# Chunked linear attention in halves of 64 tokens: units of 8 heads, column tiles, a redrawn order

## The chip, the cores and the metric
The kernel runs on one core of one Trainium2 chip. The metric is the device time of one execution in microseconds, the median of several runs. The core has TensorE (matrix products, PE in the profile, its weight loads PEld), VectorE (DVE), ScalarE (ACT), GpSimd (POOL) and SyncE (SP), which here issues every DMA.

## The reference, cut to what matters
The input is x of 4 sequences x 1024 tokens x 256 features. Three layers follow each other: half an FFN (routed to one of 8 experts by low-rank terms), an attention layer with a gated MLP, half an FFN again. Each starts from a layer norm. The change touches the recurrence of the attention, with 16 heads of 16 features:

```
def step(carry, inp):
    C, n = carry
    qt, kt, vt, it, ft = inp
    C = ft[:, :, None, None] * C + it[:, :, None, None] * (vt[..., :, None] * kt[..., None, :])
    n = ft[..., None] * n + it[..., None] * kt
    ht = jnp.einsum('bhde,bhe->bhd', C, qt)
    denom = jnp.maximum(jnp.abs(jnp.einsum('bhd,bhd->bh', n, qt)), 1.0)[..., None]
    return ((C, n), ht / denom)
```

i_gate is exp(clip(h @ wi + bi)), f_gate is sigmoid(h @ wf + bf). The result y goes through wo and is added to the layer's input; then come a norm and silu(h2 @ w_gate) * (h2 @ w_up) @ w_down.

## The kernel before, in words
Tokens go in 8 blocks of 512, two blocks a sequence, a block in 4 chunks of 128. RUNS lists the runs of work: "1" and "2" are the two FFNs, "A" the projections of the attention, "L" the gated MLP, each for one block. In the steady part a round is L of one block, 1 of the block three later, A of the block two later, 2 of the first. The attention of a block goes on between its A and its L, in steps put between those of the runs.

Every engine executes a fixed list. Its steps are generators with one-letter names, and ORDER says, for each engine, which generator takes the next step ("3U" is three steps of U). Each step waits for semaphores of the others. So what stands ahead in an engine's list must be done before what stands behind it.

On TensorE: U makes up-projections and the attention's projections into two PSUM banks (product(), lines 1044 to 1046, three matmuls of float32 halves that stand for one precise product). V makes down-projections. G transposes normed inputs and computes routing (line 1216, on column tiles of 32). S, M and Y are the attention.

The recurrence is computed by chunks. A unit is 4 heads of a chunk (QUAD, NQ = 4 units a chunk, 128 units in all).
- E (SP) broadcasts the running products of the forget gates from DRAM to the tile dm, on all partitions. D (VectorE, line 979) turns them by a scan into the matrix of decay between tokens, 128 x 512.
- S (TensorE, line 1236) multiplies keys and queries, one 128 x 128 matrix a head, in bfloat16 parts stacked to 96 rows. P (VectorE, line 990) multiplies by dm into pt.
- M (TensorE, line 1255) multiplies pt by the gated values with one more column for the denominator (vp, 17 columns), on four column tiles of 32 tokens. After the fourth unit the state of the chunks before is added to the same bank M by two full-width matmuls (line 1269, carry) with q scaled by cumE; a chunk that opens a sequence has none.
- Y: wv (GpSimd, line 562) is vp weighted by the decay to the chunk's end. Line 1282 multiplies k by wv, all heads with all heads, into bank W; lines 1004 and 1007 (VectorE) mask the blocks of a head with itself; lines 576 and 581 (GpSimd) decay the old state and add the new. A chunk that closes a sequence makes no state. Then VectorE divides (lines 1012 to 1022, y), TensorE transposes y (line 1289), ScalarE and VectorE split it (lines 757 and 1026), TensorE multiplies by wo (the same lines 1044 to 1046), VectorE adds it to z (line 1030). One bank W serves state, transpose and output product of a chunk, so the next state waits for z.

The forget products are scanned over 128 tokens at line 875; the input gate is one exp on ScalarE for a block, and vp is written at line 881, one instruction for two chunks. r_h and r_l are the two halves of an FFN's hidden activations: ScalarE writes r_h (line 624), VectorE r_l (line 807), and V waits for both. u_st holds the low-rank part of an FFN's input in two buffers.

Of the kernel before, what the change touches and what calls it, by code (L numbers as in the profile page):

```python
# [7 lines left out]
P = 128  # L8
N_SEQ, SEQ, D = 4, 1024, 256
TILES = 4  # L10
# [5 lines left out]
F = 1024  # L16
# [10 lines left out]
NQ = H // QUAD  # L27
UNITS = TILES * NQ
# [37 lines left out]
class Run:  # L66


    def __init__(self, i):
# [19 lines left out]
        2G 2U 2G 3U V 2U V U V U V 4U V 2U V U 2V 2G 6U G 2U 2G U G 7U V 2U V U V U V 3U 2S U V 2U V U V 2S 2M Y V 2S 2M S Y M S M G Y S G 2U S M 2U M 2U S M  # L89
        Y U S G U Y 2M G S Y U S 2M U G U S U M G Y 3U Y U S V M U M U Y V 2M U M V Y U V Y 2U Y U 2S U V 2U V G U V 2S 2M V 2U G 2U V 2U 2S 3M V 2U V G 2S Y  # L90
        2U G Y M V U G U V U S G M Y M V 4U V 2U V U V U V 3U G U V 2U V U G 2V 2U S 2U S M 2U G S Y U M U M Y G M S M Y S 2M G U Y G 2U S 3U S U M U V U M Y
        U V M Y M U M V U V Y 2U Y U S U V 2U V G U V S V 2U G 2U V 2U V S 2U V S M G M Y 2U G V U G U V U G 2S 2M V 4U V 2U V U V U V 3U G U V 2U V U G 2V 2U
        S 2U S Y 2U G 2M U Y 2S 2M U G M Y 2S G Y 2M G U Y U S U S U 2M 2U 2S M Y 2U V Y M U M U Y V 2M U M V Y U V Y 2U Y 2U V 2U V U V G 2S Y V 2U G 2U V 2U
        V 2U V 2S 2M G 2U G S V U G U V U G S 3M V 4U V 2U V U V U V 3U G U V 2U V U G 2V 2U S 2U S Y 2U G 2M U Y 2S 2M U G Y M 2S G M Y M G U Y U S U S 3U 3M
        Y S U S U V M U M Y U V M Y M U M V U V Y 2U Y 2U V 2U V U V G 2S V 2U G 2U V 2U 2S V 2U V 2M Y G 2U G 2S V U G U V U G 2M V 4U V 2U V U V U V 3U G U
        V 2U V U G 2V 2U S 2U S Y 2U G M U M Y S M S U M G M Y 2S G Y 2M G U Y 2U S U M 3U Y S 2M U S Y V M 2U S M Y V M U V 2M Y U V Y 3U S Y U V 2U V U V G
        2S M V 2U G 2U V 2U V 2U V 2S 2M G 2U G S V U G U V U G S 2M V 3U Y U V 2U V U V U V 3U G U V 2U V U G 2V 2U S 2U Y M 2U G S M U Y S M U M Y G M 2S M
        Y G M G 2U S U Y U S 2U 3M Y 2U 2S V M U M Y U V M Y M U M V U V Y 3U S Y U V 2U V U V S G V S 2U G S U M U M V 2U S M V U V U G 2U V 2U G V 2U S V S
        Y M 4U S Y 2M U S M U G S M S M G Y S Y U G Y 2M 2U G U Y S M 3U Y U S 2M V 2U S Y M S M V Y S M U V S 2M Y U V U Y U S U Y S U M V M S 2U M V G S 2M
        S U V Y U S V Y 2M U S Y M U Y G S 2M U V S M Y 2U S M Y V 2U S M V Y S M S M U M Y U V S M Y U 3M U Y V Y V G 4U G U V U V U V U G 2U G V U G U V U G  # L100
# [1236 lines left out]
```

## Time and profile before

| | us |
|---|---|
| median of 3 runs | 987.48 (985.0 to 989.41) |
| the profiled execution | 983.92 |
| its span on the core | 982.1 |
| TensorE busy | 904.4 |
| VectorE busy | 716.5 |
| ScalarE busy | 353.3 |
| GpSimd busy | 247.2 |

The span reaches from the first to the last instruction. A busy time is the union of an engine's instructions, waiting left out. Matmuls overlap each other, so the mean of one is longer than what it takes from the engine; where costs count, starts are compared. A float32 matmul stands in the records twice, a bfloat16 or float32r one once. A granted clock of 1.00 is the upper of TensorE's two levels, 2.4 GHz; the lower is 1.2 GHz.

### The profile page before, as it was taken

How to read it: one execution, taken by the hardware profiler on the slowest of the kernel's cores; microseconds unless marked ns; L12 is line 12 of the kernel's file. 1: busy time of each engine (PE TensorE's matmuls, PEld its weight loads, DVE VectorE, ACT ScalarE, POOL GpSimd, SP SyncE). 2: the span in 40 equal slices, each digit the busy share in tenths (PEclk: the TensorE clock that was granted, in tenths of full speed). 3: DMA queues.
4: the chain of work that ended last, by engine and by line, in shares of the span. 5: the costliest groups of instructions: out<-in, count | busy, mean ns of one | idle time of the engine just before them, and what ended most of it. 6: DMA issues, size and time to landing. Idle time of an engine off the chain costs nothing.

```text
span 982.1 us, 29559 instructions
## 1 busy us (share of the span) xinstructions
PE 904.4 (92%) x12008; PEld 865.6 (88%) x12008; DVE 716.5 (73%) x1516; ACT 353.3 (36%) x692; POOL 247.2 (25%) x285
## 2 busy tenths in 40 slices
PE   3957889999899998999999999999999989997998
PEld 2857889999789997999889997999989978987998
DVE  6634798985857859786787859887688888895642
ACT  5452251433415352343514433252423341313431
POOL 1021252320431123321412304411323143411100
PEclk9877989999999999999999999999999989998999
DMA  8105455220452126330462105531353156510000
GB/s 289 56 16 147 130 148 150 76 74 5 124 139 69 52 61 167 104 85 23 120 172 85 51 24 157 148 90 30 83 161 119 36 161 175 152 46 1 2 21 23
DMA packets 73077, 92.67 MB, mean 94 GB/s; under 512 B 10638, under 2 KB 47246, under 8 KB 72944
## 3 DMA queue, kind: packets, MB, share of 16 engines
q1 hardware_dynamic: 72944, 90.80, 33.0%
q8 instruction: 96, 1.57, 0.7%
q14 instruction: 37, 0.30, 0.1%
HBM read 73.46 MB, written 17.30 MB: 92 GB/s over the span
## 4 chain that ended last, share of the span: by engine, by line
PE 69%; DVE 11%; SPq 8%; issue 6%; DMA 3%; ACT 2%; POOL 1%; DVEq 0%; ACTq 0%; POOLq 0%
PE bank L1044 19%; PE bank L1046 18%; PE bank L1045 18%; SPq L425 5%; PE bank L1079 3%; PE bank L1255 3%; PE bank L1202 2%; PE bank L1236 2%; DMA dm<-f_scratch 2%; DVE dm L979 2%; SPq L443 1%; PE bank L1269 1%; DVE pt L990 1%; PE bank L1282 1%; DVE a_st L892 1%
## 5 line engine op out<-in xcount | busy, mean ns | idle before, releaser
L624 ACT ACTIVATE r_h<-bank 128x512 fp32r<-128x512 f32 x128 | 76.4, 598 | 280.3 <-PE bank L1079 280.2
L979 DVE TENSOR_TENSOR_SCAN dm<-dm,ident 128x512 f32<-128x512 f32 x128 | 159.7, 1254 | 22.9 <-DMA dm<-f_scratch 22.6
L1044 PE MATMUL bank<-wo_hi,r_h 128*128 128x256 f32 x512 | 147.2, 287 | 4.3 <-DVE r_l L807 4.0
L1044 PE MATMUL bank<-xT_hi,wi_hi 128*128 128x256 f32 x512 | 148.6, 290 | 1.9 <-DVE r_l L807 1.5
L1045 PE MATMUL bank<-wo_hi,r_l 128*128 128x256 f32 x512 | 144.5, 282 | 0.0
L1046 PE MATMUL bank<-wo_lo,r_h 128*128 128x256 f32 x512 | 144.4, 282 | 0.0
L1046 PE MATMUL bank<-xT_lo,wi_hi 128*128 128x256 f32 x512 | 144.4, 282 | 0.0
L1045 PE MATMUL bank<-xT_hi,wi_lo 128*128 128x256 f32 x512 | 144.2, 282 | 0.0
L807 DVE SCALAR_TENSOR_TENSOR r_l<-bank,r_h 128x512 fp32r<-128x512 f32 x128 | 87.5, 684 | 77.4 <-ACT r_h L624 76.8
L562 POOL TENSOR_TENSOR wv<-vp,dm 128x68 f32<-128x68 f32 x128 | 49.8, 399 | 245.9 <-DVE dm L979 132.5
L1044 PE MATMUL bank<-xT_hi,wgu_hi 128*128 128x256 f32 x352 | 102.7, 292 | 2.4 <-DVE xT_lo L941 2.1
L1044 PEld LDWEIGHTS bank<-wo_hi,r_h 128*128 128x128 f32 x512 | 97.2, 190 | 5.5 <-issue 5.2
L1044 PEld LDWEIGHTS bank<-xT_hi,wi_hi 128*128 128x128 f32 x512 | 97.7, 191 | 3.8 <-DVE r_l L807 3.3
L1045 PE MATMUL bank<-xT_hi,wgu_lo 128*128 128x256 f32 x352 | 99.6, 283 | 0.0
L1046 PE MATMUL bank<-xT_lo,wgu_hi 128*128 128x256 f32 x352 | 99.4, 282 | 0.0
L1045 PEld LDWEIGHTS bank<-xT_hi,wi_lo 128*128 128x128 f32 x512 | 97.8, 191 | 0.0
L1046 PEld LDWEIGHTS bank<-xT_lo,wi_hi 128*128 128x128 f32 x512 | 97.5, 190 | 0.0
L1046 PEld LDWEIGHTS bank<-wo_lo,r_h 128*128 128x128 f32 x512 | 97.3, 190 | 0.0
L1045 PEld LDWEIGHTS bank<-wo_hi,r_l 128*128 128x128 f32 x512 | 97.2, 190 | 0.0
L990 DVE TENSOR_TENSOR pt<-bank,dm 128x512 f32<-128x512 f32 x128 | 85.7, 681 | 10.4 <-PE bank L1255 9.1
L519 POOL TENSOR_TENSOR g_rs<-g_ve,minus_half 128x4 f32<-128x4 f32 x24 | 29.2, 1216 | 230.4 <-DVE g_ve L920 218.5
L1044 PEld LDWEIGHTS bank<-xT_hi,wgu_hi 128*128 128x128 f32 x352 | 67.5, 192 | 3.6 <-issue 1.7
(158 smaller groups left out, 2198.7 us busy)
## 6 DMA issues: line engine op xcount, KB each, us to landing
dm<-f_scratch SPq DMA_DIRECT2D x128, 256.0 KB, 4.4
arena<-parts_scratch SPq DMA_DIRECT2D x96, 128.0 KB, 3.5
arena<-parts_scratch SPq DMA_DIRECT2D x96, 64.0 KB, 3.7
arena<-parts_scratch SPq DMA_DIRECT2D x32, 192.0 KB, 3.9
x<-in_x SPq DMA_DIRECT2D x16, 256.0 KB, 3.0
parts_scratch<-pa SPq DMA_DIRECT2D x64, 64.0 KB
parts_scratch<-pb SPq DMA_DIRECT2D x64, 64.0 KB
parts_scratch<-pc SPq DMA_DIRECT2D x64, 64.0 KB
```

The source lines that it names most:

```text
L425: sp.dma_start(to, part[:, x % 2, jj * DC * P:(jj + 1) * DC * P]).then_inc(d_parts[x % 2], 16)
L519: nc.gpsimd.tensor_tensor(g_rs[:], g_ve[:], minus_half[:, 0:TILES], ALU.pow).then_inc(g_rstd, 1)
L562: nc.gpsimd.tensor_tensor(wv[:, heads], vp[:, b % 2, j, heads], w, ALU.mult).then_inc(a_wv, 1)
L624: nc.scalar.activation(flat(r_h[:, n]), U[use % 2][:], ACT.Relu).then_inc(f_rh, 1)
L807: v.scalar_tensor_tensor(r_l[:, n].rearrange("p a t -> p (a t)"), U[use % 2][:], 0.0, r_h[:, n].rearrange("p a t -> p (a t)").bitcast(F32) ...
L979: v.tensor_tensor_scan(dm[:, g], dm[:, g], ident4[:], 0.0, ALU.mult, ALU.add).then_inc(a_D, 1)
L990: v.tensor_tensor(pt[:, u % 2], S[u % 2][:], dm[:, u % NQ], ALU.mult).then_inc(a_P, 1)
L1044: nc.tensor.matmul(dst, lh, rh, start=first, stop=False, **more)
L1045: nc.tensor.matmul(dst, ll, rh, start=False, stop=False, **more)
L1046: return nc.tensor.matmul(dst, lh, rl, start=False, stop=last, **more)
L1079: done = nc.tensor.matmul(dst, lora_b[0:LS2, cols], u_st[0:LS2, r.k % 2, h * HALF:(h + 1) * HALF], start=False, stop=True, skip_group_chec ...
L1255: done = nc.tensor.matmul(M[tile, h * HV:(h + 1) * HV], pt[:, u % 2, i * P + q * P // COLS:i * P + (q + 1) * P // COLS], vp[:, b % 2, j, h ...
```

## The change
A chunk of 128 tokens is split into two halves of 64 (TH). Decay, scores and values are made within a half; what the second half takes from the first goes through the state. A unit is now 8 heads of a chunk (GH), 64 units in all. In bank S, partitions 0 to 63 hold the first half and 64 to 127 the second, each head 64 columns.
- S: for each head four matmuls on column tiles of 32 keys, with the 64 queries of their own half.
- M: heads in pairs; two tiles take one head, two the other, and the values vq have both halves side by side with zeros in the other half's rows, 34 columns. The clearing of vq is one memset on GpSimd at the start. There are three buffers of two chunks.
- The forget products are scanned and stored by halves, the input gate is four small exp instructions a block instead of one, the value product two instructions of 64 partitions instead of one.
- State: k by wv on four column tiles, each with its own two heads, 68 columns, for every chunk. VectorE makes from it the state at the chunk's half (c_at[1]) and at its end (c_at[0]), two small instructions each. GpSimd spreads each by head (c_ex) under the mask.
- Carry: for each half four column tiles x two groups of features, so 16 matmuls of 68 columns a chunk, 8 in an opening one. It waits for this chunk's own first state and spread.
- dm has three buffers, y and u_st one; wo's rows are loaded in another order, and yT is written by halves.
- ORDER is redrawn on all engines; the steps of U, V and G are the same in number.

Core of the diff:

```
+TH = P // 2
+GH = 8
+NG = H // GH
+UNITS = TILES * NG
+DMBUFS = 3
+VBUFS = 3
...
+        vq = sb("vq", [P, VBUFS, 2, H, 2, HV])
...
+                        src = f_d[b % 2, j, :, GH * g:GH * (g + 1)].rearrange("m h t -> m (h t)")
+                        sp.dma_start(dm[:, n % DMBUFS], src.unsqueeze(1).to_broadcast([2, TH, GH * TH])).then_inc(d_fb[n % DMBUFS], 16)
...
+                nc.gpsimd.memset(vq[:], 0.0).then_inc(s_zero, 1)
...
+                        w = dm[:, n % DMBUFS].rearrange("p (h t) -> p h t", h=GH)[:, :, TH - 1:TH].to_broadcast([P, GH, 2 * HV])
...
+                def spread(n):
+                    pairs = HH // 2
+                    nc.gpsimd.tensor_tensor(c_ex[n][:].rearrange("p c (q d) -> p c q d", q=pairs),
+                                            c_at[n][:].unsqueeze(2).to_broadcast([P, DC, pairs, 2 * HV]),
+                                            headmask[:].rearrange("p (q d) -> p q d", q=pairs).unsqueeze(1).to_broadcast([P, DC, pairs, 2 * HV]),
+                                            ALU.mult).then_inc(a_ex[n], 1)
...
+                    pool.wait_ge(a_at[1], DC * (n + 1))
+                    pool.wait_ge(a_c, n)
+                    spread(1)
...
+                        pool.wait_ge(a_at[0], DC * n_on(b, j))
+                        pool.wait_ge(a_c, n + 1)
+                        spread(0)
...
+            def input_gates(b, h):
+                half = 2 * b + h
+                if half >= VBUFS:
+                    act.wait_ge(a_wv, NG * 2 * (half - VBUFS + 1))
+                    act.wait_ge(a_O, NG * 2 * (half - VBUFS + 1))
...
-                        if r.k > 1:
-                            of = FFN_RUN[r.k - 2]
+                        if r.k:
+                            of = FFN_RUN[r.k - 1]
...
+                    for c in range(DC):
+                        if opens(b, j):
+                            done = v.tensor_scalar(two(c_at[1][:, c]), added[:, c, :, 0], 1.0, None, ALU.mult)
+                        else:
+                            done = v.scalar_tensor_tensor(two(c_at[1][:, c]), two(c_at[0][:, c]), end(c, 0), added[:, c, :, 0],
+                                                          ALU.mult, ALU.add)
+                        done.then_inc(a_at[1], 1)
...
+                        for i in range(GH):
+                            h = place_of(GH * g + i)
+                            for q in range(COLS):
+                                tile = slice(q * P // COLS, (q + 1) * P // COLS)
+                                own = slice(q // 2 * TH, (q // 2 + 1) * TH)
+                                done = nc.tensor.matmul(S[n % 2][tile, i * TH:(i + 1) * TH], ks[:, j % 2, h, tile], qs[:, j % 2, h, own],
+                                                        start=True, stop=True)
...
+                        for i in range(GH // 2):
+                            pair = GH // 2 * g + i
+                            for q in range(COLS):
+                                tile = slice(q * P // COLS, (q + 1) * P // COLS)
+                                of = (2 * i + q // 2) * TH + q % 2 * (P // COLS)
+                                done = nc.tensor.matmul(M[tile, pair * 2 * HV:(pair + 1) * 2 * HV], pt[:, n % 2, of:of + P // COLS],
+                                                        values(b, j)[:, 2 * pair + q // 2].rearrange("p m d -> p (m d)"),
+                                                        start=pair == 0, stop=False, skip_group_check=True)
...
+                        pe.wait_ge(a_ex[1], c_n + 1)
+                        pe.wait_ge(a_qc, DC * (b + 1))
+                        if not opens(b, j):
+                            pe.wait_ge(a_ex[0], n_on(*chunks[c_n - 1]))
...
+                                    of = c_ex[m][:, c].rearrange("p (h e d) -> p h e d", e=2, d=HV)[:, :, q // 2]
+                                    done = nc.tensor.matmul(heads[tile, HH // 2 * c:HH // 2 * (c + 1), m], q32[:, b % 2, c, t:t + P // COLS], of,
+                                                            start=False, stop=True, skip_group_check=True)
...
+                            done = nc.tensor.matmul(W[tile, c * 4 * HV:(c + 1) * 4 * HV], k32[:, b % 2, j, of:of + P // COLS],
+                                                    wv[:, HH * c + 2 * q:HH * c + 2 * q + 2].rearrange("p h m d -> p (h m d)"),
+                                                    start=True, stop=True)
```

## Rows read from the trace of the kernel before

**Rows 1.** The page's first lines: the span, and TensorE's busy time.
```profile
span 982.1 us, 29559 instructions
...
PE 904.4 (92%) x12008; PEld 865.6 (88%) x12008; DVE 716.5 (73%) x1516; ACT 353.3 (36%) x692; POOL 247.2 (25%) x285
```

**Rows 2.** Stretches: from:to, length, busy us by engine, clock, DMA share, GB/s.
```profile
0.00:112.00 112.00, 77.01 (x652) 72.94 (x653) 62.07 (x131) 46.24 (x89) 17.85 (x20) 0.86 0.41 124
112.00:860.00 748.00, 717.57 (x10129) 686.83 (x10129) 584.14 (x1239) 272.35 (x539) 214.84 (x251) 0.98 0.37 102
```

**Rows 3.** Waits of TensorE: who waited for whom, us in total, times, longest.
```profile
PE bank L1236 <- DVE pt L990: 5.1, 4, 1.5
PE bank L1289 <- DVE y L1022: 4.4, 6, 1.2
```

**Rows 4.** Timeline, an M unit among products: start us, us, instruction, count.
```profile
758.60 0.28 PE L1046 MATMUL bank<-xT_lo,wgu_hi 128*128 128x256 f32 x1
758.81 0.45 PE L1255 MATMUL bank<-vp,pt 128*32 128x17 f32 x32
...
759.41 0.28 PE L1045 MATMUL bank<-xT_hi,wgu_lo 128*128 128x256 f32 x1
```

**Rows 5.** Timeline, an S unit among products, and two S units in a row.
```profile
605.59 0.28 PE L1046 MATMUL bank<-wkv_lo,xT_hi 128*128 128x256 f32 x1
605.72 0.40 PE L1236 MATMUL bank<-arena 96*128 96x128 bf16 x4
...
606.12 0.28 PE L1045 MATMUL bank<-xT_hi,wi_lo 128*128 128x256 f32 x1
...
536.32 0.62 PE L1236 MATMUL bank<-arena 96*128 96x128 bf16 x8
```

**Rows 6.** Timeline, a state step among products.
```profile
396.86 0.28 PE L1046 MATMUL bank<-wo_lo,r_h 128*128 128x256 f32 x1
396.98 0.62 PE L1282 MATMUL bank<-wv,k 128*128 128x136 f32 x4
...
397.56 0.28 PE L1045 MATMUL bank<-xT_hi,wi_lo 128*128 128x256 f32 x1
```

**Rows 7.** Lines 1255 and 1216: ns min/median/max, first and last start; a routing group.
```profile
L1255 PE MATMUL bank<-vp,pt x4096: 177/183/238, 112.7 to 884.0; 128*32 128x17 f32 x196
...
L1216 PE MATMUL bank<-route_w,xn x1024: 196/202/277, 19.1 to 945.4; 128*32 128x40 f32 x171
...
664.32 0.80 PE L1216 MATMUL bank<-route_w,xn 128*32 128x40 f32 x64
```

**Rows 8.** VectorE's groups by line: count, busy us, mean ns, idle us before.
```profile
L979 DVE TENSOR_TENSOR_SCAN dm<-dm,ident 128x512 f32<-128x512 f32 x128 | 159.7, 1254 | 22.9 <-DMA dm<-f_scratch 22.6
L990 DVE TENSOR_TENSOR pt<-bank,dm 128x512 f32<-128x512 f32 x128 | 85.7, 681 | 10.4 <-PE bank L1255 9.1 <-PE bank L1236 0.8
L881 DVE TENSOR_TENSOR vp<-bank,vp 128x512 f32<-128x512 f32 x16 | 10.8, 678 | 2.9 <-PE bank L1046 2.8
L1014 DVE SCALAR_TENSOR_TENSOR den<-bank,den 128x16 f32<-128x16 f32 x32 | 5.6, 175 | 1.1
```

**Rows 9.** GpSimd's groups by line, the same columns.
```profile
L562 POOL TENSOR_TENSOR wv<-vp,dm 128x68 f32<-128x68 f32 x128 | 49.8, 399 | 245.9 <-DVE dm L979 132.5 <-PE bank L1282 60.6 <-issue 33.2
L581 POOL TENSOR_TENSOR cb<-cm,cbd 128x272 f32<-128x272 f32 x24 | 18.8, 784 | 10.6 <-DVE cm L1007 6.4 <-DVE dm L979 3.4 <-issue 0.8
L576 POOL TENSOR_TENSOR cbd<-cb,cumE 128x272 f32<-128x272 f32 x24 | 16.4, 683 | 8.3 <-DVE cb L1004 3.7 <-DMA cumE<-c_scratch 2.1 <-POOL cb L581 0.4
```

**Rows 10.** Timeline of the first microseconds.
```profile
1.44 0.91 DVE L771 MEMSET u_st<- 32x1024 f32 x1 [0.27 <-issue]
...
5.69 1.02 POOL L519 TENSOR_TENSOR g_rs<-g_ve,minus_half 128x4 f32<-128x4 f32 x1 [4.85 <-DVE g_ve L920]
```

**Rows 11.** Timeline of a chunk's end: denominator to y, transpose to the split.
```profile
386.36 0.16 DVE L1012 TENSOR_SCALAR den<-bank 128x16 f32<-128x16 f32 x1
...
387.05 0.42 DVE L1022 TENSOR_TENSOR y<-bank,den 128x256 f32<-128x256 f32 x1
...
388.88 0.38 PE L1289 MATMUL bank<-ident,y 128*128 128x128 f32 x2
...
389.70 0.42 DVE L1026 TENSOR_TENSOR yT_lo<-bank,yT_hi 128x256 fp32r<-128x256 f32 x1 [0.23 <-ACT yT_hi L757]
```

More of the change, by code:

```diff
@@ L210, in build @@
         u_rep = sb("u_rep", [P, TILES, 3, ER])
[L211 removed]
+        u_st = sb("u_st", [P, BLOCK], F32R)
         r_h = sb("r_h", [P, 2, 2, HALF], F32R)
@@ L339, in build @@
         upto = lambda b, j: chunks[:b * TILES + j + 1]
-        n_carry = lambda b, j: sum(not opens(*c) for c in upto(b, j))
-        n_state = lambda b, j: sum(not closes(*c) for c in upto(b, j))
-        n_cb = lambda b, j: sum(not closes(*c) and not opens(*c) for c in upto(b, j))
+        n_on = lambda b, j: sum(not closes(*c) for c in upto(b, j))
         def n_ml(l, s):
@@ L686, in projections @@
                     act.wait_ge(d_f, 16 * TILES * b)
-                nc.scalar.copy(fTz[:, 1:P], bank(A_F)[:, 1:P]).then_inc(a_fTs, 1)
+                halves = lambda t: t.rearrange("p (m t) -> p m t", m=2)[:, :, 1:TH]
+                nc.scalar.copy(halves(fTz[:]), halves(bank(A_F)[:, 0:P])).then_inc(a_fTs, 1)
                 yield
+                input_gates(b, 1)
+                yield
+            def input_gates(b, h):
[3 more added lines that the diff above has]
+                    act.wait_ge(a_O, NG * 2 * (half - VBUFS + 1))
+                else:
+                    act.wait_ge(s_zero, 1)
+                for m in range(2):
+                    rows = slice(m * TH, (m + 1) * TH)
+                    nc.scalar.activation(vq[rows, half % VBUFS, :, :, m, HD], g32[rows, 2 * h:2 * h + 2, 0:H], ACT.Exp).then_inc(a_i, 1)
             def G_():
@@ L874, in projections @@
                     dve.wait_ge(d_c, 16 * TILES * b)
-                v.tensor_tensor_scan(cum[:], bank(A_F)[:, 0:P], zero[:].to_broadcast([P, P]), 1.0, ALU.mult, ALU.add).then_inc(f_read, 1)
+                for m in range(2):
+                    t = slice(m * TH, (m + 1) * TH)
+                    done = v.tensor_tensor_scan(cum[:, t], bank(A_F)[:, t], zero[:].to_broadcast([P, TH]), 1.0, ALU.mult, ALU.add)
+                done.then_inc(f_read, 1)
                 yield
@@ new lines, in Y_ @@
+                    yield
+                    if not closes(b, j):
+                        dve.wait_ge(d_ce, 16 * DC * (b + 1))
+                        dve.wait_ge(a_at[1], DC * (n + 1))
+                        dve.wait_ge(a_ex[0], n_on(*chunks[n - 1]) if n else 0)
+                        for c in range(DC):
+                            v.scalar_tensor_tensor(two(c_at[0][:, c]), two(c_at[1][:, c]), end(c, 1), added[:, c, :, 1],
+                                                   ALU.mult, ALU.add).then_inc(a_at[0], 1)
+                        yield
@@ L1258, in M_ @@
                         done.then_inc(a_O, 1)
                         yield
[L1260 to L1272 removed]
+                        if g < NG - 1:
+                            continue
```

345 lines of the change are left out of this document (157 added, 188 removed).

## Prediction
> **What bounds the kernel now.** I read the page's first lines, then the busy time by stage, then the waits of TensorE, then single stretches of its timeline. TensorE is busy for 904.4 of 982.1 us [rows 1]. Outside the first 112 us, where weights are still being prepared, it is busy for 717.6 of 748 us, while VectorE has 584.1 of them and ScalarE and GpSimd less [rows 2]. The largest waits of TensorE that the change touches are small: 5.1 us in all for a pt, 4.4 us for a y [rows 3]. So time goes down only by what leaves TensorE's own stream, plus or minus what its waits change; VectorE, ScalarE, GpSimd and DMA work is free as long as its results come when the fixed order asks for them.
>
> Busy time misleads for small matmuls, since they overlap. I price a step by what it takes out of a stream of products, whose starts stand 0.117 us apart: the start of the second product after it, less the start of the last one before it, less two spacings. An M unit alone (16 matmuls, two records each, on column tiles of 32): 759.41 - 758.60 - 0.234 = 0.576 us [rows 4]. An S unit of four full-width matmuls: 606.12 - 605.59 - 0.234 = 0.296 us, and two of them in a row 0.22 more, since eight records last 0.62 against 0.40, 0.055 us a matmul [rows 5]. A state step (two matmuls, four records of 136 columns): 397.56 - 396.86 - 0.234 = 0.466 us, at most 0.116 a record, 0.85 ns a column [rows 6]. Within the M group the 31 intervals take 0.45 - 0.183 = 0.267 us, 8.6 ns a record [rows 4, 7]; so 0.275 us of the 0.576 is its matmuls, and 0.30 us is paid once for going into tiles and out again. The routing step, also tiled but with 40 columns instead of 17, has (0.80 - 0.202)/63 = 9.5 ns a record [rows 7]: four tiles with 40 columns take 38 ns, where one alone needs 34 by the price per column. So four tiles overlap, and neither 17 nor 40 columns bounds them much.
>
> **The change, part by part: TensorE.** Counted in the code and the two written-out orders.
>
> Before: M has 128 units x 0.275 = 35.2 us; runs of tiled steps (M and routing) are 115 x 0.30 = 34.5; S has 82 single units and 23 pairs, 82 x 0.296 + 23 x 0.516 = 36.1; carry and state 56 x 0.466 = 26.1 (the carry has the same shape). Sum 131.9 us, without routing's own records, which stay.
>
> After, four tiles at a time. M: 64 units of 16 matmuls, now 34 columns. Between 17 and 40 columns four records take 34 to 38 ns; I take 37: 64 x 8 x 37 = 18.9 us. S: 64 units x 8 heads x four bf16 matmuls of 64 columns, one record each. Its columns would allow 28 ns (half of 55), the record pace of tiles 34; I take 34: 17.6 us. Upper bound: if the pace belongs to a matmul and not to a record, it is 0.275/16 = 17.2 ns each, 35.2 us. Carry: 28 chunks x 16 matmuls and 4 x 8, 68 columns, 58 ns for four records by columns: 28 x 0.46 + 4 x 0.23 = 13.8 us. State: 32 x 8 matmuls, 32 x 0.23 = 7.4 us, also for the closing chunks, which had none. All four kinds are tiled now, and read off the new order they form, with routing, 109 runs: 32.7 us. Sum 90.4 us. TensorE's stream loses 41.5 us, between 24 (S at its upper bound) and 46 (S by columns, M at 34 ns).
>
> U, V, projections, transposes and routing keep their counts.
>
> **VectorE.** dm scans go from 128 to 64 at 1.254 us and pt products from 128 to 64 at 0.681 [rows 8]: 123.9 us less. The value products double (16 more at 0.678, since half the partitions last as long): +10.9. 28 masks of some 0.43 go, 120 small ones on 34 columns come; nearest is the 16-column one at 0.175 [rows 8]; at 0.2 each +12 net. VectorE drops by about 101 us, from 78% to some 66% of the middle stretch. On the path that gives back only part of the waits in [rows 3]; I take 5 us, 0 to 12. The doubled value product keeps a U bank 0.68 us longer, twice per projection run, 16 x 0.68 = 11 at most; V and attention steps stand there too, so I take 3.
>
> **GpSimd and queues.** wv: 64 on 272 columns at about 0.78 [rows 9] = 50 us, as before (128 x 0.399). 48 carry operations become 60 spreads at 0.78: +10 us on an engine with 215 of 748 us busy [rows 2]; nothing queues but the chain below. The clearing of vq (3264 columns) stands before the first g_rs, which began at 5.69 [rows 10]. At VectorE's pace of 0.91 us for 1024 columns it takes 2.9 us and is over in time; at GpSimd's 2.9 ns a column 9.4 us and 4.5 late. I take 1. SP issues 64 dm loads less, at half the bytes in all; three buffers of a double unit hold 1.5 chunks instead of one. One u_st buffer: its copy on ScalarE now waits for the last U of the FFN run just before. Only the last two FFN runs are adjacent, with V steps left to cover a copy and a subtraction: 0. The second input gate waits for M of the block before, which stands 3.6 us or more ahead of it in the stream (read with the prices above), so 0; behind it the next r_h would queue.
>
> **The chain in a chunk.** This is the new wait. Before, the carry used a state made a chunk earlier. Now state matmul, VectorE's update for the first half, its update for the second, two spreads on GpSimd, carry: 0.3 + 0.4 + 2 x 0.71 + 0.1 = 2.2 us from the end of the state step (0.71 between the two nearest operations [rows 9]). Then carry to y: VectorE's four operations, 386.36 to 387.47, and the tail, 1.35 us; y transposed to its product: 388.88 to 390.12, 1.0 us past the step [rows 11]. I laid the steps of both orders in a row at their prices and looked up the work between each pair. Before, four places are short of these needs, by 2.5 us in sum; after, 23 are, by 16.7: C behind state 4.5 us in 7 places, the transpose behind C 5.5 in 7, the output product behind the transpose 5.2 in 6, the next state behind VectorE 1.5 in 3. The difference is 14 us, with bounds of 0 (a place where TensorE would have waited for something else anyway) and 30 (each hand-over also meets one VectorE instruction in progress).
>
> **Sum.** Against the profiled execution, 983.9 us: -41.5 + 14 + 3 + 1 - 5 = -28.5, so 955.4. The median of the runs is 3.6 us above that execution; with it **958 us**.
>
> **A rule that speaks against it.** The records of M stand 8.6 ns apart, 17.2 ns a matmul [rows 4, 7]. The Trainium skill, page "TensorE: Matmul & The Clock Gate", section "Wait — 56ns, not 53.3ns?", says that starts of matmuls never come closer than about 25 ns, however few the columns. The trace disagrees. By that rule 32 matmuls of an S unit would take 0.8 us instead of 0.275, 34 us more over the kernel, and the result would be 992 us, near the second rival's.
>
> **Rivals.**
> 1. The chain turns it round, slower. Place: the C step of a chunk, waiting for GpSimd's second spread. What speaks for it: seven places leave it less than 2.2 us, and VectorE is busy for two thirds of the time, so a hand-over often finds a 0.68 us instruction ahead. Against it: in the middle blocks the order leaves 3 to 23 us there. If each chunk meets two such instructions more than forecast on hand-overs without cover, 32 x 1.36 = 43.5: **1002 us**. It decides from (987.5 - 958)/32 = 0.92 us a chunk.
> 2. The tiles of S do not overlap. M and routing, the only tiled rows, stream the same operand to all four tiles; S streams another to each pair, and no row shows that. Then 32 x 28 ns = 0.90 us a unit, 64 x 0.62 = 40 us more: **998 us**.
> 3. It does not do what it says: the saved matmul time becomes idle, because the stream was held by the loop U, r_h, r_l, V. The idle share, 4% outside the start, speaks against it: **987 us**.
> 4. The waits shrink with VectorE's load instead of growing: chain 0, relief 12: **937 us**.
>
> **How the numbers follow.** Forecast 0.65, with its own range 938 to 976 from the bounds of S and of the chain. Rival 1 0.10, rival 2 0.05, rival 3 0.10, rival 4 0.10. 0.5% of 987.5 is 4.9 us, about what a measurement of this kernel can tell from no change. Faster: forecast and rival 4, and a little of rival 3, 0.76; same: the rest of rival 3 and a tail of the forecast, 0.10; slower: rivals 1 and 2, less what falls within 0.5%, 0.14. The range 932 to 990 takes in forecast, rivals 3 and 4, and leaves out rivals 1 and 2 and the tails.
>
> **What would show it.** In the profile after: S, M, C and state in TensorE's lines as 2048, 2048, 960 and 512 records; an S unit alone at about 0.58 us (right) or above 1.1 (rival 2); TensorE busy near 863 us; waits of C for the spread, of the y transpose and of the output product at some 15 us in sum (right) or above 40 (rival 1); VectorE near 615 us. I am wrong if tiled matmuls with different streams take turns, if carry and state cost more than 58 ns for four, or if TensorE's idle time grows by over 30 us.

## The result and the profile of the changed kernel

The changed kernel takes 1038.58 us (median of 4 runs, 1033.04 to 1040.67), the kernel before 986.91: ratio 1.051 (95% interval 1.046 to 1.056). It was forecast at 958 us, and the range ended at 990; none of the rivals was the cause. The sign that the prediction had named for being wrong, TensorE's idle time growing by over 30 us, is there. The profiled execution is 1038.6 us against 982.1 [rows 1].

The changed kernel's page, first lines, then its span and mean granted clock:

```profile
span 1038.6 us, 30736 instructions
...
PE 890.4 (86%) x12744; PEld 846.2 (81%) x12744; DVE 627.3 (60%) x1502; ACT 358.7 (35%) x716; POOL 244.5 (24%) x234
```

```profile
core 0: 1038.6 us, clock 0.939
```

TensorE's busy time fell by 14.0 us [rows 1], VectorE's by 89.2 (forecast 101). But the time in which TensorE is not busy rose from 982.1 - 904.4 = 77.7 us to 148.2. So the question is what it waits for. Its waits first, then VectorE's (who waited for whom, us in total, times, longest):

```profile
PE bank L1289 <- DMA arena<-parts_scratch: 27.1, 4, 10.7
PE bank L1092 <- DVE yT_lo L1073: 20.4, 9, 7.4
PE bank L1092 <- DVE r_l L835: 19.8, 12, 4.9
PE bank L1264 <- DVE xT_lo L976: 13.4, 7, 6.0
...
PE bank L1329 <- POOL c_ex L584: 0.9, 2, 0.6
```

```profile
DVE r_l L835 <- ACT r_h L643: 86.8, 61, 4.9
DVE dm L1012 <- DMA dm<-f_scratch: 67.1, 22, 7.3
```

The spread (c_ex) that rival 1 feared costs 0.9 us. r_l, yT_lo and xT_lo are VectorE's results, and VectorE has less to do than before; but it stands for 67.1 us at a dm scan (L1012) that waits for its load, where it stood 22.6 before [rows 8], and everything behind that scan in its order stands too. S (L1289) waits 27.1 us for arena, the loads of keys and queries, which the change doesn't touch. Both point at DMA. The groups of the dm scan and of S show the same from the other side (count, busy us, mean ns, idle us before):

```profile
L1012 DVE TENSOR_TENSOR_SCAN dm<-dm,diag 128x512 f32<-128x512 f32 x64 | 78.6, 1229 | 67.2 <-DMA dm<-f_scratch 67.1
L1289 PE MATMUL bank<-arena 96*32 96x64 bf16 x2048 | 29.5, 202 | 27.2 <-DMA arena<-parts_scratch 27.1
```

Next the chain that ended last, in order of time (start, us, step), and a stretch in which nearly nothing but one dm load is under way (from:to, length, busy us by engine, clock, DMA share, GB/s):

```profile
361.06 12.50 DMA dm<-f_scratch
...
776.34 17.39 DMA dm<-f_scratch
```

```profile
364.00:370.00 6.00, 6.00 (x53) 5.96 (x52) 3.02 (x10) 1.20 (x2) 1.65 (x1) 1.00 0.14 53
```

The DMA engines are busy for 0.14 of their time; 0.14 x 16 = 2.2. One dm load keeps two of the 16 busy, at 53 GB/s, for many microseconds. In the code it is one DMA whose source is given as [2, TH, GH * TH]: the two halves outermost, since each half of the partitions now reads another row. The destination is written as dm's 128 partitions, which take the rows in that order; where the expectations below say "destination of 2 x 64", it is this shape. Before, both sides were [128, 512], one row to all. Of the loads that stand alone in the trace, from the start of the issue to the end of the last packet, it takes about 7 us (6.5 to 7.2) with two packets moving at a time (2.0 to 2.1), before 2.7 us with 6.1 to 9.1 (the expectations below have 2.4 and 2.35 for it).

The updates of the loads' own semaphores say the same without a count of packets. A load before has 16 of them. A load of the changed kernel has three: one about 1 us after the issue, before its first packet (at 1.3 us), and two at the end, 6.9 us after it or later. So two parts of the load finish on their own where there were 16.

### The profile page after: what moved, and what is told of

Read it like the earlier page. It is cut to its first block, busy times and chain, and to the rows that moved or that the text cites. A ratio compares the mean times of both kernels' runs of the same rounds, so it can differ in the third digit from the quotient of the medians.

```text
span 1038.6 us, 30736 instructions
## 1 busy us (share of the span) xinstructions
PE 890.4 (86%) x12744; PEld 846.2 (81%) x12744; DVE 627.3 (60%) x1502; ACT 358.7 (35%) x716; POOL 244.5 (24%) x234
## 4 chain that ended last, share of the span: by engine, by line
PE 48%; DMA 16%; issue 15%; SPq 8%; DVE 7%; ACT 3%; POOL 2%; ACTq 0%; DVEq 0%; POOLq 0%
PE bank L1092 14%; PE bank L1093 12%; PE bank L1094 12%; DMA dm<-f_scratch 9%; SPq L438 4%; DMA parts_scratch<-pc 2%; DMA arena<-parts_scratch 2%; SPq L456 2%; PE bank L1250 2%; PE bank L1127 2%; DMA f_scratch<-fTz 1%; DMA c_scratch<-cum 1%; PE bank L1310 1%; PE bank L1329 1%; PE bank L1289 1%
## 5 line engine op out<-in xcount | busy, mean ns | idle before, releaser
L1092 PE MATMUL bank<-wo_hi,r_h 128*128 128x256 f32 x512 | 151.2, 295 | 19.4 <-DVE r_l L835 17.4
L1093 PE MATMUL bank<-wo_hi,r_l 128*128 128x256 f32 x512 | 147.2, 288 | 0.0
L1012 DVE TENSOR_TENSOR_SCAN dm<-dm,diag 128x512 f32<-128x512 f32 x64 | 78.6, 1229 | 67.2 <-DMA dm<-f_scratch 67.1
L1092 PEld LDWEIGHTS bank<-wo_hi,r_h 128*128 128x128 f32 x512 | 100.0, 195 | 23.4 <-issue 19.8
L1093 PEld LDWEIGHTS bank<-xT_hi,wi_lo 128*128 128x128 f32 x512 | 100.5, 196 | 0.0
L1093 PEld LDWEIGHTS bank<-wo_hi,r_l 128*128 128x128 f32 x512 | 100.3, 196 | 0.0
L1094 PEld LDWEIGHTS bank<-wo_lo,r_h 128*128 128x128 f32 x512 | 100.2, 196 | 0.0
L584 POOL TENSOR_TENSOR c_ex<-c_at,headmask 128x272 f32<-128x272 f32 x60 | 44.9, 748 | 190.1 <-DVE c_at L1042 92.4
L577 POOL TENSOR_TENSOR wv<-vq,dm 128x272 f32<-128x272 f32 x64 | 43.1, 677 | 192.4 <-PE bank L1344 91.2
L1250 PE MATMUL bank<-ident,xn 128*128 128x128 f32 x256 | 44.0, 299 | 29.3 <-ACT xn L732 12.1
```

The costliest lines, as they stand in the source:

```text
L577: nc.gpsimd.tensor_tensor(wv[:, heads].rearrange("p h m d -> p h (m d)"), values(b, j)[:, heads].rearrange("p h m d -> p h (m d)"), w, ALU ...
L584: nc.gpsimd.tensor_tensor(c_ex[n][:].rearrange("p c (q d) -> p c q d", q=pairs), c_at[n][:].unsqueeze(2).to_broadcast([P, DC, pairs, 2 * HV]),
L1012: v.tensor_tensor_scan(dm[:, n % DMBUFS], dm[:, n % DMBUFS], diag[:], 0.0, ALU.mult, ALU.add).then_inc(a_D, 1)
L1092: nc.tensor.matmul(dst, lh, rh, start=first, stop=False, **more)
L1093: nc.tensor.matmul(dst, ll, rh, start=False, stop=False, **more)
L1094: return nc.tensor.matmul(dst, lh, rl, start=False, stop=last, **more)
```

## Experiments

**The load in two DMAs.** The changed kernel with the same bytes in the same place, one DMA for each half, so that the outermost size is 64:

```diff
-sp.dma_start(dm[:, n % DMBUFS], src.unsqueeze(1).to_broadcast([2, TH, GH * TH])).then_inc(d_fb[n % DMBUFS], 16)
+for m in range(2):
+    sp.dma_start(dm[m * TH:(m + 1) * TH, n % DMBUFS], src[m].partition_broadcast(TH)).then_inc(d_fb[n % DMBUFS], 16)
...
```

The dots stand for the waits, which count 32 where they counted 16.

> The changed kernel with one edit: each decay load goes out as two DMAs, one for each half of 64 partitions, instead of one whose outer size is 2. Theory A (the load's shape): the traces show the packets of a load overlapping 2 at a time and landing some 7 us after the issue, where before they overlapped 6 to 11 at a time and landed after 2.4 us; that keeps VectorE at the scan (67 us of waits) and delays the key and query loads behind it (27 us of TensorE waits for arena). Then landing falls to 2 to 3 us, these two waits to under 25 and under 8 us, and the time to 950 to 985 us. Theory B (the chain within a chunk, state, spreads, carry, y): the load is beside the point, the waits of TensorE at the output product stay near 20 us, and the time stays above 1020 us. Theory C (order redrawn for other durations): the waits move elsewhere, 1000 to 1030 us.

Measured: 947.65 us (942.43 to 948.54), ratio to the kernel before 0.959 (0.956 to 0.963). The same kernel was measured a second time:

> The changed kernel with two dm loads of 64 partitions once more, on the chip of the run beside it, as the base of the comparisons: the ratio to the kernel before was 0.9592 (0.9555 to 0.963), so 944 to 951 us again.

It was 945.4 us, ratio 0.958 (0.954 to 0.961). So 91 us hang on the shape of one load. Each of the two loads of 64 partitions has 16 updates of its semaphore, as the load before had. Of the first of the two runs: the page's busy times, the dm scan's group, TensorE's waits, and the load's issues (KB each, median us from the start of an issue to the semaphore's last update):

```profile
PE 866.7 (92%) x12744; PEld 824.7 (87%) x12744; DVE 628.5 (66%) x1502; ACT 358.4 (38%) x716; POOL 246.3 (26%) x234
```

```profile
L1013 DVE TENSOR_TENSOR_SCAN dm<-dm,diag 128x512 f32<-128x512 f32 x64 | 79.1, 1240 | 1.3 <-DMA dm<-f_scratch 1.3
```

```profile
PE bank L1093 <- DVE yT_lo L1074: 6.0, 7, 1.7
PE bank L1354 <- DVE y L1070: 5.3, 7, 1.4
PE bank L1290 <- DMA arena<-parts_scratch: 4.3, 2, 2.5
...
PE bank L1330 <- POOL c_ex L585: 1.7, 3, 0.8
...
PE bank L1345 <- DVE z L1079: 1.0, 2, 0.5
```

```profile
dm<-f_scratch SPq DMA_DIRECT2D x128, 128.0 KB, 3.0
```

The wait for dm is 1.3 us instead of 67.1. That for arena is 4.3 instead of 27.1, though its loads are as they were: they had been queued behind the slow ones. In the changed kernel the three long waits for arena (10.4, 10.7 and 5.4 us) end with loads that were issued 5 to 8 us behind a dm load and took 9.0 to 9.9 us to land; here the longest such wait, 2.5 us, ends with one that took 4.4.

The narrow load costs in two ways. Of the 92.9 us between the two spans (1038.6 and 945.7), 69.2 are time in which TensorE isn't busy (148.2 against 79.0). The other 23.7 are busy time (890.4 against 866.7) for the same matmuls, at a mean granted clock of 0.939 against 0.977: TensorE stood still more often and was granted the lower clock for more of the time.

**The kernel before with the narrow shape.** f stored twice, and each dm load from two (equal) rows to 2 x 64 partitions; nothing else changed:

```diff
...
-sp.dma_start(dm[:, g], f_d[b % 2, j, QUAD * g:QUAD * (g + 1)].rearrange("h t -> (h t)").partition_broadcast(P)
-             ).then_inc(d_fb[g], 16)
+src = f_d[b % 2, j, :, QUAD * g:QUAD * (g + 1)].rearrange("m h t -> m (h t)")
+sp.dma_start(dm[:, g], src.unsqueeze(1).to_broadcast([2, P // 2, QUAD * P])).then_inc(d_fb[g], 16)
```

> The kernel before with the decay load in the form of the change: the products are stored twice, and each load of 256 KB goes to partitions as 2 x 64, from two rows. Nothing else changes, 128 loads remain. Theory A: 64 packets of 84 ns one after the other on each of two DMA engines is 5.4 us a load at least, 690 us in sum; TensorE waits for pt and for arena, and the time is over 1050 us. Theories B and C: under 1000 us.

Measured: 1365.42 us (one run). VectorE's wait for dm:

```profile
DVE dm L979 <- DMA dm<-f_scratch: 385.5, 107, 12.8
```

With 128 loads instead of 64 the same shape costs 379 us (against 986.18 for the kernel before, measured beside it). The cause lies in the load and not in the order or in the halves.

**Two narrow DMAs.** Is it the outermost size, or that a single DMA was too big?

```diff
-sp.dma_start(dm[:, n % DMBUFS], src.unsqueeze(1).to_broadcast([2, TH, GH * TH])).then_inc(d_fb[n % DMBUFS], 16)
+for k in range(2):
+    part = slice(k * GH * TH // 2, (k + 1) * GH * TH // 2)
+    sp.dma_start(dm[:, n % DMBUFS, part], src[:, part].unsqueeze(1).to_broadcast([2, TH, GH * TH // 2])).then_inc(d_fb[n % DMBUFS], 16)
...
```

> The changed kernel, where each dm load is cut in two DMAs by columns: 256 of the 512 columns each, both still with a destination of 2 halves x 64 partitions. It issues as many DMAs as the kernel with two loads of 64 partitions (947.65 us), of the same size in all, and differs from it in the outermost size of each alone. Theory A, the outermost size of 2 holds a DMA to about two packets at a time: the two DMAs share the same two engines, packets are half as long and twice as many, so a dm comes no earlier than in the changed kernel, 7 us after its issue or more: 1030 to 1090 us, and fewer than 3 packets of dm in flight. Theory B, a DMA of 256 KB has too little in flight and any cut in two cures it: 945 to 960 us.

Measured: 1066.25 us (two runs), ratio 1.082 (1.073 to 1.091). Two DMAs cure nothing if each has an outermost size of 2; the wait for dm is 82.0 us, and each DMA has three updates of its semaphore. Theory B falls.

**Outermost size 4.** f stored in four rows, the source 4 x 32 rows, one DMA:

```diff
-sp.dma_start(dm[:, n % DMBUFS], src.unsqueeze(1).to_broadcast([2, TH, GH * TH])).then_inc(d_fb[n % DMBUFS], 16)
+sp.dma_start(dm[:, n % DMBUFS], src.unsqueeze(1).to_broadcast([4, TH // 2, GH * TH])).then_inc(d_fb[n % DMBUFS], 16)
...
```

> The changed kernel, where f is stored twice (two stores for each chunk instead of one), so that one dm load has a destination of 4 x 32 partitions instead of 2 x 64; one DMA for a dm as in the changed kernel. Theory A, the outermost size is the number of packets that move at once (2 in the changed kernel at 7.1 us from issue to landing, 1038.6 us): with 4 the landing is half, some 3.5 to 4 us, about the 2.35 us of the kernel before plus one; most of the wait for dm goes, 950 to 975 us, and 3 to 4 packets in flight. Theory B, any outermost dimension other than the 64 or 128 rows is slow alike: above 1020 us. The 16 more stores of f cost SP some 1 us in all and nothing on the path.

Measured: 980.36 us, ratio 0.994 (0.991 to 0.997). Of the waits for dm 21.1 us are left, and those for arena are 15.5:

```profile
L1013 DVE TENSOR_TENSOR_SCAN dm<-dm,diag 128x512 f32<-128x512 f32 x64 | 79.6, 1247 | 21.1 <-DMA dm<-f_scratch 21.1
```

A load that stands alone takes 4.1 us, with four packets at a time (3.9 to 4.0) and five updates of its semaphore. So outermost size 2, 4, 64 (64 as two DMAs) gives about 7, 4.1 and 3.0 us from issue to landing, and 1038.6, 980.4 and 947.65 us. The time is 5 us above my interval, since I took a load of 4 us for nearly hidden; the direction and the packets are theory A's. (There are 32 more stores of f, one a chunk, not 16.) Whether more dm buffers would have hidden the narrow load wasn't tried.

**VectorE's work given back.** With the load cured, what is the term "VectorE does 101 us less, relief 5 us" worth? Behind each dm scan, two products of a 0/1 matrix with itself:

```diff
...
 v.tensor_tensor_scan(dm[:, n % DMBUFS], dm[:, n % DMBUFS], diag[:], 0.0, ALU.mult, ALU.add).then_inc(a_D, 1)
+dve.wait_ge(a_D, n + 1)
+for k in range(2):
+    dve.wait_ge(a_more, 2 * n + k)
+    v.tensor_tensor(diag[:], diag[:], diag[:], ALU.mult).then_inc(a_more, 1)
```

> The kernel with two dm loads of 64 partitions (947.65 us, 0.9592 of the kernel before), with VectorE's saved work given back: two products of 512 columns (the 0/1 matrix times itself) behind each dm scan, 128 x about 0.65 = 83 us, so VectorE is busy for some 711 us, against 729 before and 628 without them. It prices the term of the sum 'VectorE does 101 us less, relief 5 us, 0 to 12'. If the term is right: 5 x 83/101 = 4 us, 948 to 958 us. Rival: that kernel came 10 us below the forecast because the relief was worth three times the term: 12 to 20 us, 960 to 968 us. If VectorE had become the bound without the relief: above 985 us.

Measured: 1027.84 us, ratio 1.043 (1.038 to 1.049): far above the term and its rival, in the interval that I had kept for VectorE as the bound (above 985 us). The products lasted 0.84 us instead of 0.65, and r_l is late (busy times, the products' group, a wait of TensorE):

```profile
PE 888.4 (87%) x12744; PEld 841.0 (82%) x12744; DVE 732.0 (71%) x1630; ACT 357.9 (35%) x716; POOL 262.5 (26%) x234
```

```profile
L1020 DVE TENSOR_TENSOR diag<-diag 128x512 f32<-128x512 f32 x128 | 107.2, 838 | 4.4
```

```profile
PE bank L1100 <- DVE r_l L837: 27.5, 18, 3.8
```

But VectorE is busy for 732 us of 1024, and the kernel before has 716.5 us of such work and needs 987, so the amount of its work isn't the bound. Of the 80 us, 22 are TensorE's own busy time (888.4 against 866.7), at a mean clock of 0.957 against 0.977. Next the same work in other places, one product behind each scan and one behind each pt product (more() waits for the last one and does the next):

```diff
...
 v.tensor_tensor_scan(dm[:, n % DMBUFS], dm[:, n % DMBUFS], diag[:], 0.0, ALU.mult, ALU.add).then_inc(a_D, 1)
+more()
...
 v.tensor_tensor(pt[:, n % 2], S[n % 2][:], dm[:, n % DMBUFS], ALU.mult).then_inc(a_P, 1)
+more()
```

> The run with the load given back to VectorE cost 80 us for 107 us of work, in 64 places of 1.25 + 2 x 0.84 = 2.9 us that nothing can interrupt. Here is the same work (128 products of 0.84 us), one behind each dm scan and one behind each pt product: 64 places of 2.1 us and 64 of 1.5. Theory A, VectorE's amount of work is what counts: 1020 to 1035 us again. Theory B, what counts is what an urgent instruction (r_l, xT_lo, y) finds ahead of it in one piece, whose mean grows with the square of the places: (64 x (2.1^2 + 1.5^2) - 64 x (1.25^2 + 0.68^2)) / (64 x (2.9^2 + 0.68^2) - 64 x (1.25^2 + 0.68^2)) = 0.67 of the 80 us, 1001 us (990 to 1010).

Measured: 1002.19 us (999.13 to 1005.9), ratio 1.016 (1.011 to 1.021); TensorE's wait for r_l is shorter:

```profile
PE bank L1109 <- DVE r_l L837: 16.7, 18, 2.7
```

The same 128 products cost 55 us instead of 80. That fits theory B, by which what counts is what an urgent result finds ahead of it in one piece; the squares of the pieces gave 1001. One run fits the formula; that it holds elsewhere isn't shown, nor that it is the length of the pieces and not their new places. In both runs GpSimd's busy time rose as well, from 246.3 us to 262.5 and 262.9; how much of the 80 and the 55 us comes through it wasn't separated.

**VectorE's saving alone, in the kernel before.** Scans and pt products on half their columns, so half of each pt is old data:

```diff
-v.tensor_tensor_scan(dm[:, g], dm[:, g], ident4[:], 0.0, ALU.mult, ALU.add).then_inc(a_D, 1)
+v.tensor_tensor_scan(dm[:, g, 0:QUAD * P // 2], dm[:, g, 0:QUAD * P // 2], ident4[:, 0:QUAD * P // 2], 0.0, ALU.mult, ALU.add).then_inc(a_D, 1)
...
-v.tensor_tensor(pt[:, u % 2], S[u % 2][:], dm[:, u % NQ], ALU.mult).then_inc(a_P, 1)
+half = slice(0, QUAD * P // 2 if n > 1 else QUAD * P)
+v.tensor_tensor(pt[:, u % 2, half], S[u % 2][:, half], dm[:, u % NQ, half], ALU.mult).then_inc(a_P, 1)
```

> The kernel before, where each dm scan and each pt product does only its first 256 of 512 columns (the other half of the dm isn't cumulated and the other half of each pt is old data; the counts and all else stay). VectorE loses about what the change removes from these two: 128 x 0.63 + 128 x 0.34 = 124 us, 605 us busy instead of 729. It prices the relief term of the sum in the order of the kernel before. If the term (5 us, 0 to 12) is right: 975 to 987 us. Rival, the relief is worth 15 to 35 us: 951 to 971 us.

Measured: 976.7 us, ratio 0.990 (0.987 to 0.993), 9.8 us less; VectorE went down by 84 us only, from 716.5 to 632.4. At that rate 101 us give 12, the upper bound of the term, not 5. (The change with the load cured took 88 us off VectorE, 716.5 to 628.5, not 101.)

**TensorE's saving alone, and both.**

```diff
-                        for i in range(QUAD):
+                        for i in range(QUAD // 2 if n > 1 else QUAD):
                             h = place_of(QUAD * g + i)
...
-                        for i in range(QUAD):
+                        for i in range(QUAD // 2 if n >= NQ else QUAD):
                             h = QUAD * g + i
```

> The kernel before, where each S unit and each M unit does two of its four heads (from the third unit and the second chunk on; the other heads of a pt and of M hold old data). TensorE's stream loses 126 x 2 x 0.055 = 13.9 us of S and 124 x 8 x 0.0172 = 17.1 us of M, 31 us. If the stream sets the time, as the forecast has it: 952 to 960 us. Rival 3 (the saved time becomes idle, because the loop U, r_h, r_l, V holds the stream): 975 to 987 us.

Measured: 975.44 us, ratio 0.987 (0.983 to 0.992): 31 us leave the stream, 11 come through. The number is that of rival 3; then the cuts of VectorE and of TensorE together:

> The kernel before with both cuts at once: dm scans and pt products of 256 columns (alone: 976.7 us, 9.8 less than before) and S and M units of two heads (alone: 975.44, 11.1 less, where the stream loses 31 us); the other halves hold old data. Theory A, the two savings are separate and add up: 9.8 + 11.1 = 21 us less, 962 to 970 us. Theory B, the 20 us of the stream's saving that did not come through were held by VectorE's results (r_l, pt, u_rep), and come through once VectorE has less to do: 31 + 10 = 41 us less, 941 to 952 us.

Measured: 965.12 us, ratio 0.976 (0.972 to 0.981): 22.8 less, they add up within what the intervals allow, and theory B falls. Then where did the rest of the 31 us go? Busy times and mean clock of the run with VectorE's cut alone, then of the run with both:

```profile
PE 895.1 (92%) x12008; PEld 855.4 (88%) x12008; DVE 632.4 (65%) x1516; ACT 352.8 (36%) x692; POOL 230.3 (24%) x285
```

```profile
core 0: 975.3 us, clock 0.979
```

```profile
PE 882.1 (91%) x9772; PEld 839.4 (87%) x9772; DVE 634.6 (66%) x1516; ACT 352.8 (37%) x692; POOL 230.9 (24%) x285
```

```profile
core 0: 964.1 us, clock 0.959
```

Busy time fell by 13.0 us only. Times the mean clock it is 895.1 x 0.979 = 876.3 and 882.1 x 0.959 = 845.9, a difference of 30.4, the stream's saving as counted (31). The mean clock is that of the whole span, so this is an estimate; for the kernel before and the run with TensorE's cut alone (886.5 us at 0.958) the same working gives 23.4. In between lies the clock: all four runs with the thinner stream beside less VectorE work have 0.959 to 0.966, the four without it 0.970 to 0.981; with TensorE's cut alone the four have 0.958 to 0.960, the seven of the kernel before 0.967 to 0.976. The lower level was granted for some 78 us of the span with both cuts, against 41 with VectorE's cut alone. One place where it happens, at a block's end, with both cuts:

```profile
360.00:364.00 4.00, 2.80 (x106) 1.95 (x105) 3.76 (x14) 1.20 (x3) 1.97 (x4) 1.00 0.49 137
364.00:368.00 4.00, 2.32 (x12) 1.68 (x13) 3.69 (x11) 2.14 (x5) 1.42 (x2) 0.86 0.82 248
368.00:372.00 4.00, 4.00 (x21) 3.91 (x21) 3.75 (x8) 0.22 (x1) 1.47 (x2) 0.50 0.54 130
```

and the same place with VectorE's cut alone:

```profile
364.00:368.00 4.00, 3.18 (x138) 2.48 (x138) 3.79 (x13) 1.80 (x4) 1.97 (x4) 1.00 0.59 154
368.00:372.00 4.00, 2.44 (x40) 1.59 (x29) 3.66 (x11) 1.91 (x5) 1.33 (x2) 1.00 0.59 193
372.00:376.00 4.00, 3.52 (x33) 3.30 (x33) 3.90 (x9) 0.45 (x1) 1.56 (x3) 1.00 0.79 206
```

TensorE is busy for 2.80 and 2.32 of 4 us, then runs at 0.50, which is 1.2 GHz, though there is work; with VectorE's cut alone 3.18, 2.44 and 3.52 leave the clock at 1.00. But the clock fell at this place in the kernel before too, whose stream is full, behind 4 us in which TensorE was busy for 2.07:

```profile
372.00:376.00 4.00, 3.49 (x15) 3.00 (x16) 3.97 (x9) 2.37 (x5) 2.18 (x3) 0.58 0.89 241
```

So the place alone shows that a thin stretch can lose what it saved, not that each such loss comes from the cut; that the thinner stream is granted less is shown by the clocks of all the runs above.

**The chain in a chunk.** Each spread done twice:

```diff
...
+for mark in (a_tw, a_ex):
+    if mark is a_ex:
+        pool.wait_ge(a_tw[n], times)
     nc.gpsimd.tensor_tensor(c_ex[n][:].rearrange("p c (q d) -> p c q d", q=pairs),
...
```

> The kernel with two dm loads of 64 partitions (947.65 us), where GpSimd does each of the 60 spreads (c_ex) twice, one behind the other: 0.75 us more for each, 45 us more work on GpSimd and 1.5 us more between a chunk's state step and its carry. It tells how much of the chain in a chunk lies on the path. Forecast's theory (a few chunks have too little work between; 7 places of 32 were short of 2.2 us): 8 to 12 places pay up to 1.5 us, 8 to 18 us more, 956 to 966 us, and TensorE's waits for c_ex go from 1.7 to some 10 us. Rival 1 (each chunk meets it): 32 x 1.5 = 48 us, 990 us or more. Third, the chain is covered everywhere: 947 to 950 us.

Measured: 951.99 us, ratio 0.964 (0.958 to 0.971), between the third answer and the forecast's. GpSimd went from 246.3 to 292.2 us and the wait for c_ex from 1.7 to 4.5:

```profile
PE bank L1334 <- POOL c_ex L589: 4.5, 6, 1.4
```

Most chunks hide even 1.5 us more. Rival 1, with 48 us, is out.

**The start.** TensorE's order begun as before:

```diff
-        3G U G 4U V U V
+        2G 2U 2G 3U V U V
...
```

> The kernel with two dm loads of 64 partitions (947.65 us), with TensorE's order begun as in the kernel before: 2G 2U 2G 3U instead of 3G U G 4U; the rest of the order is unchanged. In the former the first projection product starts at 19.05 us, because the first routing step stands ahead of it and waits 4.3 us for xT_lo; in the kernel before it started at 14.91. Theory A, those 4 us are on the path: 943 to 946 us, and the wait of 4.3 us is gone. Theory B, the start is set by the weights, which are still being prepared until about 100 us: no change, 947 to 949 us.

Measured: 947.13 us, ratio 0.960 (0.956 to 0.964): no change, theory B. The first projection's delay isn't on the path.

## Why the prediction was wrong, point by point

**The step that failed** stands under "GpSimd and queues": "SP issues 64 dm loads less, at half the bytes in all". I counted issues and bytes and took no price for the shape. The line is in the diff, and no row of the kernel before has a load of such a shape, so it called for a bound from both sides. The packets of the changed kernel's loads take some 84 ns each; 128 of them two at a time are 5.4 us, for a load that a pt waits for. What the runs showed in place of a term of 0 is 91 us (1038.58 against 947.65).

The Trainium skill, page "DMA: Bandwidth & Descriptors", section "Why a DMA increments its semaphore by 16 and not by 1", has the rule: the number of DMA engines that a DMA uses is the largest up to 16 that divides the outermost sizes of both of its patterns. By that rule 2, 4 and 16 here (16 for each of the two loads of 64). The traces agree: 2.0 to 2.1 and 3.9 to 4.0 packets at a time for the first two, and three, five and 16 updates of a load's semaphore. With two loads of 64, 6 to 9 packets move at a time, so the packets alone would not show the 16. The same page's "Rules for kernel authors" advise one transfer over two to disjoint halves of the partitions. Measured here, the two are 91 us faster, because the one had the halves outermost.

**TensorE's stream.** With the load cured its records in the trace, a single S and a single M unit:

```profile
621.99 0.27 PE L1095 MATMUL bank<-xT_lo,wgu_hi 128*128 128x256 f32 x1
622.20 0.42 PE L1290 MATMUL bank<-arena 96*32 96x64 bf16 x32
622.54 0.38 PE L1093 MATMUL bank<-xT_hi,wgu_hi 128*128 128x256 f32 x1
622.76 0.28 PE L1094 MATMUL bank<-xT_hi,wgu_lo 128*128 128x256 f32 x1
...
732.79 0.28 PE L1095 MATMUL bank<-xT_lo,wgu_hi 128*128 128x256 f32 x1
733.00 0.46 PE L1311 MATMUL bank<-vq,pt 128*32 128x34 f32 x32
733.39 0.39 PE L1093 MATMUL bank<-xT_hi,wgu_hi 128*128 128x256 f32 x1
733.62 0.28 PE L1094 MATMUL bank<-xT_hi,wgu_lo 128*128 128x256 f32 x1
```

By the forecast's own measure S is 622.76 - 621.99 - 0.234 = 0.536 us (forecast 0.58), M 733.62 - 732.79 - 0.234 = 0.596 (0.59). Rival 2 is out: 32 matmuls of S start within 622.54 - 622.20 = 0.34 us, 11 ns each at most. The Trainium skill, page "TensorE: Matmul & The Clock Gate", section "Wait — 56ns, not 53.3ns?", has about 25 ns as the least distance between starts, the rule that the prediction weighed; the trace disagrees for these column tiles, with its 11 ns. A carry measured the same way is 0.82 (forecast 0.76), a state step 0.57 (0.53). With these the sum after is about 91 us against 90.4. Busy time fell by 904.4 - 866.7 = 37.7, forecast 41.5. But the mean clock rose, from the kernel before to the load-cured one:

```profile
core 0: 982.1 us, clock 0.965
```

```profile
core 0: 945.7 us, clock 0.977
```

That is 904.4 x 0.012 = 11 us of the 37.7, and busy time times clock fell by 872.7 - 846.8 = 26 only. With the clock taken over TensorE's busy time alone, the traces give 876.9 us for the kernel before and 848.3 for the load-cured one, 28.6 less; the same matmuls read 880.6 in the kernel before with less VectorE work, so this is good to some 4 us. The prices of single units held, yet the whole stream's saving was some 30 us and not 41.5, nearer to the lower bound of 24. Which part of the tally is too high I didn't settle.

**Idle time.** The forecast had +14 chain, +3 value product, +1 start, -5 relief, together +13; measured, with the load cured, 79.0 us not busy against 77.7, +1.3. The chain's waits (yT_lo, y, c_ex, z) are 6.0 + 5.3 + 1.7 + 1.0 = 14.0 us, but the kernel before had 4.4 for y at the same step [rows 3] and 2.7 more, so the chain added some 7, half of the term. Those 2.7, waits of the kernel before:

```profile
PE bank L1255 <- DVE y L1022: 2.4, 3, 0.9
...
PE bank L1282 <- DVE z L1030: 0.3, 1, 0.3
```

The relief was worth about 12 instead of 5. The clearing of vq took 2.82 us and ended 2.9 us before GpSimd's next input was there, so 0 instead of 1; rows of the load-cured kernel:

```profile
0.77 2.82 POOL L518 MEMSET vq<- 128x3264 f32 x1
6.50 1.03 POOL L536 TENSOR_TENSOR g_rs<-g_ve,minus_half 128x4 f32<-128x4 f32 x1 [2.92 <-DVE g_ve L956]
```

**So the forecast without the failed step** (958, against 947.65 and 945.4) is 10 to 13 us high, inside its own range of 938 to 976, and partly by errors that cancel: less from the stream, more from waits and clock. That is luck in part. (Its last addition is off by one: 955.4 + 3.6 is 959.) The end of its first paragraph, that VectorE's work is free as long as it comes in time, hid a second flaw: 80 and 55 us for the same added work show how near to late it is.

## What to carry to other kernels

When a change gives two groups of partitions different data in one load, look at which dimension of the DMA is outermost, and cut it so that each DMA has the partitions outermost; a DMA share near 2/16 while a load is awaited is the sign. Price every DMA whose shape changes, even if its bytes shrink. A late load costs clock as well as waits (0.939 against 0.977 here). And take a saving in TensorE's stream times the clock that its thinner stretches will be granted. A side engine's busy share doesn't tell what more work on it costs; the length of its pieces may tell more, for which one run speaks here.

## What the runs showed of the hardware

- Outermost size 2, 4, 64 of a 256 KB load (64 as two DMAs): about 7, 4.1, 3.0 us from issue to landing, with three, five, 16 updates of a DMA's semaphore; 128 KB halves by columns with outermost size 2 don't help (1066.25 us). Loads of other tensors issued behind a narrow one are late too: TensorE's waits for arena 27.1 us against 4.3.
- Four column tiles of 32 with two different moving operands, each shared by two tiles, overlap as those with one shared by all do: 11 ns a matmul at most, for 64 columns of bf16.
- Taking 31 us of matmuls out of the stream gave 11 us alone and 13 beside less VectorE work; the granted clock fell from 0.979 to 0.959 in the pair of profiles above.
- For the same matmuls, TensorE was busy 890.4 us at a mean clock of 0.939 in the changed kernel, and 866.7 at 0.977 with the load cured.
